# Exponentials over three PSUM banks, with two score buffers, in the attention stage that takes no maximum

## What is computed

```python
Q = (x @ W_k.T).reshape(B, S, H, dk).transpose(0, 2, 1, 3)
sq_norm = sum(Q * Q, axis=-1, keepdims=True)
scores = -(sq_norm - 2 * Q @ Q^T + sq_norm^T) / sqrt(dk)
attn = softmax(scores, axis=-1)
context_q = attn @ Q
```

## Time and profile before

| what | us |
|---|---|
| median of three runs | 1814.68 |
| lowest and highest run | 1811.52, 1815.87 |
| span of the profiled execution, first to last instruction | 1808.7 |
| TensorE busy in it | 1623.3 |
| ScalarE busy in it | 1295.9 |
| VectorE busy in it | 1230.8 |

### The profile page before, as it was taken

One profiled execution on the slowest core, in us unless ns is written; L12 is line 12 of the kernel. 1 busy time (PEld: TensorE's weight loads), 2 busy tenths in 40 slices (PEclk: granted clock), 3 DMA queues, 4 the chain that ended last, 5 costly groups with the idle time before them and its releaser, 6 DMA issues. The chain is left out here.

```text
span 1808.7 us, 39123 instructions
## 1 busy us (share of the span) xinstructions
PE 1623.3 (90%) x14558; PEld 775.2 (43%) x14558; DVE 1230.8 (68%) x2499; ACT 1295.9 (72%) x2201; POOL 362.4 (20%) x660
## 2 busy tenths in 40 slices
PE   7999896874899999989899999788866999999998
PEld 4676674751233333337533333255431333333356
DVE  4677777799899999947601111146767999999743
ACT  5555653794688888876689999667763888888863
POOL 4422423732000000014300000023420000000152
PEclk9889988885899999999989999899976999999999
DMA  4000000045222222200131111002242222222101
GB/s 125 1 1 1 1 1 1 1 142 183 68 77 79 72 73 78 79 6 19 48 95 57 56 56 56 1 22 69 74 122 81 57 58 61 63 59 57 30 7 42
DMA packets 115393, 98.52 MB, mean 54 GB/s; under 512 B 26763, under 2 KB 105413, under 8 KB 115205
## 3 DMA queue, kind: packets, MB, share of 16 engines
q1 hardware_dynamic: 114148, 95.68, 18.6%
q10 hardware_dynamic: 1056, 0.33, 0.1%
HBM read 63.82 MB, written 31.59 MB: 53 GB/s over the span
## 5 line engine op out<-in xcount | busy, mean ns | idle before, releaser
L1615 ACT ACTIVATE m_probs<-m_psum 128x512 f32<-128x512 f32 (+1 forms) x768 | 513.8, 758 | 97.7 <-PE m_psum L1532 92.7
L1615 ACT ACTIVATE e_probs<-e_psum 128x512 f32<-128x512 f32 x512 | 277.2, 597 | 85.6 <-PE e_psum L1532 80.6
L1659 DVE TENSOR_REDUCE a_minus_max<-e_psum 128x1 f32<-128x512 f32 x512 | 315.8, 684 | 19.6 <-PE e_psum L1541 18.3
L1659 DVE TENSOR_REDUCE a_minus_max<-m_psum 128x1 f32<-128x512 f32 x512 | 316.0, 684 | 18.0 <-PE m_psum L1541 16.4
L1532 PE MATMUL m_psum<-m_q_stack,m_k_stack 114*32 114x512 bf16 (+1 forms) x4096 | 295.7, 385 | 13.3 <-issue 6.9
L1552 PE MATMUL m_psum<-m_probs,m_v_ones 128*32 128x512 f32 x2048 | 271.0, 601 | 2.3 <-ACT m_probs L1615 1.6
L1532 PEld LDWEIGHTS m_psum<-m_q_stack,m_k_stack 114*32 114x32 bf16 (+1 forms) x4096 | 102.4, 96 | 218.2 <-issue 129.8
L1532 PE MATMUL e_psum<-e_q_stack,e_k_stack 126*32 126x512 bf16 x2048 | 159.0, 385 | 10.4 <-issue 8.3
L1504 POOL CAST a_max_parts<-a_minus_max 128x16 bf16<-128x16 f32 x64 | 12.6, 196 | 658.8 <-DVE a_minus_max L1659 658.8
L1552 PE MATMUL e_psum<-e_probs,e_v_ones 128*32 128x512 f32 x1024 | 133.7, 595 | 0.9 <-ACT e_probs L1615 0.8
L1541 PE MATMUL m_psum<-m_k_stack,m_q_stack 48*128 48x512 bf16 x512 | 113.4, 399 | 17.0 <-DVE a_minus_max L1659 16.9
(11 more groups left out here) (426 smaller groups left out, 2770.9 us busy)
## 6 DMA issues: line engine op xcount, KB each, us to landing
polar_q<-m_late SPq DMA_DIRECT2D x24, 256.0 KB, 3.0
polar_k<-m_late SPq DMA_DIRECT2D x24, 256.0 KB, 3.3
m_q_stack<-polar_q SPq DMA_DIRECT2D x64, 96.0 KB, 2.3
m_k_stack<-polar_k SPq DMA_DIRECT2D x64, 96.0 KB, 2.3
m_q_stack<-dist_parts SPq DMA_DIRECT2D x192, 32.0 KB
m_k_stack<-dist_parts SPq DMA_DIRECT2D x192, 32.0 KB
gate_parts<-e_late SPq DMA_DIRECT2D x24, 256.0 KB, 3.0
e_q_stack<-gate_parts SPq DMA_DIRECT2D x64, 72.0 KB
```

The costliest lines, as they stand in the source:

```text
L1615: act.activation(self.buf.probs[(NT * m + c) % self.buf.PROBS][:, self.WIDE * part:self.WIDE * (part + 1), :], self.ps_s[i % self.PAIRS], ...
L1659: dve.tensor_reduce(self.minus_max[n % 2][:, k:k + 1], ps[:, :], AX.X, ALU.max, negate=True).then_inc(self.bank_free, 1)
```

## The change

In `a5` alone, a unit becomes three tiles (1536 columns over three banks), counted on across chunks and groups: 170 units of three tiles and a last one of two, 171 in all. There are two score buffers of three banks (banks 4-6 and 0-2), the products go to bank 7, the turned context stays in bank 3. The scores of unit i wait for the exponential of unit i - 2. TensorE's order is now in `tensor_wide`: the scores of unit i, then the products of the chunk that ended in unit i - 2, if one did. The ring of exponentials keeps its twelve tiles, but as one tensor, so that a unit can lie across two chunks; ScalarE now waits for earlier products before each unit. `a3` and `a7` keep units of one tile and their order.

```diff
-        self.probs = [sb(f"probs{c}", [P, GH, T]) for c in range(self.PROBS)]
+        self.probs_row = sb("probs", [P, self.PROBS * GH, T])
+        self.probs = [self.probs_row[:, c * GH:(c + 1) * GH, :] for c in range(self.PROBS)]
...
-        self.WIDE = 1 if self.with_max else 2
-        self.PER = GH // self.WIDE
-        self.UNITS = self.PER * NT
+        self.WIDE = 1 if self.with_max else 3
+        self.PER = GH
...
+    def units_to(self, m):
+
+        return -(-self.TILES * m // self.WIDE)
...
-        wait_ge(sp, self.scores_done, self.UNITS * (n - self.buf.SLOTS + 1))
+        wait_ge(sp, self.scores_done, self.units_to(n - self.buf.SLOTS + 1))
...
+    def tiles_of_unit(self, i):
+        return range(self.WIDE * i, min(self.WIDE * (i + 1), self.TILES * self.N))
+
+    def unit(self, pe, i):
         wait_ge(pe, self.exp_done, i - self.PAIRS + 1)
...
+        for j, f in enumerate(self.tiles_of_unit(i)):
+            m, c, h = f // self.TILES, f // GH % NT, f % GH
+            g = m % self.buf.SLOTS
+            if not self.with_max and f % self.TILES == 0:
+                pe.wait_ge(self.loaded[g], 16 * self.LOADS * (m // self.buf.SLOTS + 1))
...
     def pv(self, pe, m, c):
-        pe.wait_ge(self.exp_done, self.UNITS * m + self.PER * (c + 1))
+        pe.wait_ge(self.exp_done, (self.TILES * m + GH * c + GH - 1) // self.WIDE + 1)
...
+    def products(self, pe, unit):
+
+        for chunk in range(NT * self.N):
+            if (GH * chunk + GH - 1) // self.WIDE == unit:
+                m, c = divmod(chunk, NT)
+                self.pv(pe, m, c)
+                if c == 1 and m >= 1 and m % 2 == 0:
+                    self.turn_ctx(pe, m - 1)
+
+    def tensor_wide(self, pe, m):
+        for i in range(self.units_to(m), self.units_to(m + 1)):
+            self.unit(pe, i)
+            self.products(pe, i - 2)
...
     def scalar(self, act, m):
-        for v in range(self.UNITS):
-            i = self.UNITS * m + v
-            c, part = divmod(v, self.PER)
+        RING = self.buf.PROBS * GH
+        for i in range(self.units_to(m), self.units_to(m + 1)):
+            tiles = self.tiles_of_unit(i)
             act.wait_ge(self.scores_done, i + 1)
-            if part == 0:
-                wait_ge(act, self.pv_done, NT * m + c - self.buf.PROBS + 1)
-            act.activation(self.buf.probs[(NT * m + c) % self.buf.PROBS][:, self.WIDE * part:self.WIDE * (part + 1), :],
-                           self.ps_s[i % self.PAIRS], ACT.Exp).then_inc(self.exp_done, 1)
+            if not self.with_max or i % GH == 0:
+                wait_ge(act, self.pv_done, (tiles[-1] - RING) // GH + 1)
+            at = tiles[0] % RING
+            act.activation(self.buf.probs_row[:, at:at + len(tiles), :], self.ps_s[i % self.PAIRS][:, 0:len(tiles), :], ACT.Exp).then_inc(self.exp_done, 1)
...
-        second = Attention(nc, sv, "a5", buf, psum, ((4, 6, 0), 2, (3,)), l1a_loads(sv), rows=6 * DH + 6, before=between)
+        second = Attention(nc, sv, "a5", buf, psum, ((4, 0), 7, (3,)), l1a_loads(sv), rows=6 * DH + 6, before=between)
...
-                    second.tensor(pe, s)
+                    second.tensor_wide(pe, s)
```

More of the change, by code:

```diff
@@ L1449, in bank_done @@
         else:
-            eng.wait_ge(self.exp_done, self.UNITS * self.N)
+            eng.wait_ge(self.exp_done, self.units_to(self.N))
+    def units_to(self, m):
+        return -(-self.TILES * m // self.WIDE)
     def context_done(self, eng, b):
@@ L1456, in stacks_done @@
     def stacks_done(self, eng):
-        eng.wait_ge(self.scores_done, self.UNITS * self.N)
+        eng.wait_ge(self.scores_done, self.units_to(self.N))
     def load(self, sp, n):
@@ L1519, in bank @@
         return self.ps_r[r % self.BANKS]
-    def unit(self, pe, m, v):
-        c, part = divmod(v, self.PER)
-        i = self.UNITS * m + v
+    def tiles_of_unit(self, i):
+        return range(self.WIDE * i, min(self.WIDE * (i + 1), self.TILES * self.N))
+    def unit(self, pe, i):
         wait_ge(pe, self.exp_done, i - self.PAIRS + 1)
@@ L1527, in unit @@
                 self.before.bank_done(pe, self.scores[i] + j)
-        g = m % self.buf.SLOTS
-        for j in range(self.WIDE):
-            h = self.WIDE * part + j
+        for j, f in enumerate(self.tiles_of_unit(i)):
[3 more added lines that the diff above has]
+                pe.wait_ge(self.loaded[g], 16 * self.LOADS * (m // self.buf.SLOTS + 1))
             for r in range(0, P, 32):
@@ L1568, in turn_max @@
         last.then_inc(self.bank_full, 1)
+    def products(self, pe, unit):
[9 more added lines that the diff above has]
+            self.products(pe, i - 2)
     def tensor(self, pe, s):
-        n, m, PER = s, s - self.LAG, self.PER
-        tiles = self.with_max and n < self.N
+        n, m = s, s - self.LAG
+        tiles = n < self.N
         if n < self.N:
             pe.wait_ge(self.loaded[n % self.buf.SLOTS], 16 * self.LOADS * (n // self.buf.SLOTS + 1))
-        if self.with_max and m >= 0:
+        if m >= 0:
             pe.wait_ge(self.rows_loaded, 32 * (m + 1))
         for c in range(NT):
-            for i in range(0, PER, 2):
+            for i in range(0, GH, 2):
                 if m >= 0:
-                    self.unit(pe, m, PER * c + i)
-                    self.unit(pe, m, PER * c + i + 1)
+                    self.unit(pe, self.TILES * m + GH * c + i)
+                    self.unit(pe, self.TILES * m + GH * c + i + 1)
                 if tiles and i == 0:
@@ L1584, in tensor @@
                         self.tile(pe, n, 4 * c + j)
-            if self.with_max and c == 1 and 1 <= s <= self.N:
+            if c == 1 and 1 <= s <= self.N:
                 self.turn_max(pe, s - 1)
@@ L1594, in tensor_end @@
     def tensor_end(self, pe):
-        self.pv(pe, self.N - 1, NT - 1)
+        if self.with_max:
+            self.pv(pe, self.N - 1, NT - 1)
+        else:
+            for unit in range(self.units_to(self.N) - 2, self.units_to(self.N)):
+                self.products(pe, unit)
         self.turn_ctx(pe, self.N - 1)
@@ L1608, in scalar @@
     def scalar(self, act, m):
-        for v in range(self.UNITS):
-            i = self.UNITS * m + v
-            c, part = divmod(v, self.PER)
+        RING = self.buf.PROBS * GH
+        for i in range(self.units_to(m), self.units_to(m + 1)):
+            tiles = self.tiles_of_unit(i)
             act.wait_ge(self.scores_done, i + 1)
-            if part == 0:
-                wait_ge(act, self.pv_done, NT * m + c - self.buf.PROBS + 1)
-            act.activation(self.buf.probs[(NT * m + c) % self.buf.PROBS][:, self.WIDE * part:self.WIDE * (part + 1), :],
-                           self.ps_s[i % self.PAIRS], ACT.Exp).then_inc(self.exp_done, 1)
-            if self.with_max and v == self.PER and m >= 1 and m % 2 == 0:
+            if not self.with_max or i % GH == 0:
+                wait_ge(act, self.pv_done, (tiles[-1] - RING) // GH + 1)
+            at = tiles[0] % RING
+            act.activation(self.buf.probs_row[:, at:at + len(tiles), :], self.ps_s[i % self.PAIRS][:, 0:len(tiles), :], ACT.Exp).then_inc(self.exp_done, 1)
+            if self.with_max and i - self.units_to(m) == GH and m >= 1 and m % 2 == 0:
                 self.evacuate(act, m - 1)
```

## The result

The changed kernel takes 1817.22 us (median of 20 runs, 1813.35 to 1821.19), the kernel before beside it 1814.49 (median of 20, 1804.11 to 1817.87). The ratio is 1.0018, with a 95% interval of 1.0009 to 1.0026: 3.3 us slower, 1.6 to 4.7. Fewer and longer exponentials made the kernel a little slower, as forecast, and by about the forecast amount; how much of that agreement is luck is said further down.

The account below looks back on a forecast made before the run. ACT was taken to bound most of a5, PE close behind. Terms -5.3 + 4.3 + 1.3 + 2.5 = +2.8 us on the 1808.7 us span, plus 6.0 us carried over to the median, gave 1817.5 us; range 1808 to 1824.

Parts of the forecast that it names:

- Fewer exponentials: ACT in a5: 171 exponentials in place of 256 save 0.062 us fixed part each, -5.3 us.
- Two buffers: Score buffers in a5: PE falls 0.53 us behind against 0.32 slack, four units take 5.41 or 5.55 us, +4.3 us.
- Transposes: PE in a5, 15 times: with smaller slack each delays the stage 0.67 us instead of 0.6, +1.3 us.
- copy: Pair boundaries in a5: products wait for VectorE's copy of the sums, ten of 15 stall PE 0.46 us, +2.5 us.
- added waits, ring and loads: a5: ACT's wait for products before every unit and later stack loads are already covered, 0 us.
- The start: Beginning of a5: bank waits move but are covered by the DMA that first scores await, 0 us.
- Six groups 46.5: Sign in a5: six groups should take 46.5 us.
- The 0.2 us of one exponential in four: Sign in a5's steady cycles: ACT should idle some 0.2 us before one exponential in four.
- scores would wait some 37 times: Sign in a5: PE's scores should wait for ACT some 37 times.
- A: Rival for a5: two buffers suffice and PE's own pace rules, -5.9 us, total 1808.8 us; chance 0.17.
- B: Rival for a5: each PE wait costs 0.1 us beyond its length, +7.6 us in all, total 1822.3 us; chance 0.14.
- C: Rival for ACT in a5: third bank costs like its own instruction, fixed part 0.124 us, +8.1, total 1822.8 us; chance 0.05.

Follow-up runs that it names:

- Two_tiles_two_buffers: Changed kernel with units of two tiles and only two score buffers of two banks; a5 267.7 us, total 1836.33 us in one run.
- bare kernels: a5's transposes, sum copies and divisions left out of the changed kernel (238.0 us) and of its version with two-tile units and three buffers (239.2 us).
- bare_wide: Changed kernel with a5's transposes, copies of the sums and divisions left out, three-tile units and two buffers kept; a5 238.0 us, total 1800.17 us.
- Two_tiles_two_behind: Changed kernel with two-tile units and three buffers again, sums in bank 2, new code kept; a5 248.4 us, ratio 1.0001 to the kernel before.
- sums_alternate: Changed kernel with each pair's sums in bank 7 or 3 by turns, so products skip the copy wait; a5 247.7 us, ratio 0.9979 to before.
- turn_in_gap: Changed kernel with the four transposes moved behind the scores of the next unit without products; a5 247.7 us, ratio 0.9976 to the kernel before.

## Why the prediction was right

Total: 1817.5 forecast, 1817.22 measured; a5 +2.8 forecast, +2.7 measured. The mechanism held: ACT saves its fixed parts, and two buffers, the transposes and the copy cost more than that. The closeness of the numbers is in part luck, as the parts show:

1. *Fewer exponentials, -5.3.* The fixed part stands: exponentials of 1536 columns add 1.344 and last 1.45 alone.
2. *Two buffers, +4.3.* Two_tiles_two_buffers shows that buffers bite. The two bare kernels give the sum of this term and the one above, -1.2 where -1.0 was forecast, and their rows of exponentials give this one alone, 4.2. The picture behind it was only half right: 5.41 us for four units was meant for undisturbed cycles and 5.55 for those after a disturbance. In bare_wide, where nothing disturbs, the two alternate to the end (steps of 1.34, 1.34, 1.34, 1.38 and 1.34, 1.34, 1.34, 1.51), so their mean held for another reason.
3. *Transposes +1.3 and copy +2.5.* Their sum is 13.3 - 9.3 = +4.0 by the bare kernels, +3.8 forecast. After the change each was priced well: transposes 9.7 measured and 15 x 0.67 = 10.05 forecast, copy 3.6 and 3.6. Two slips lie on the side of before. The 0.6 us of a pair (15.27 against 14.67) already holds whatever the copy cost, and 1.1 us for the copy was set beside it; the trace of before has 15 long steps of 1.52 us in place of 0.92, together 9.1 us, and behind the start no other loss. And 15 x (0.67 - 0.6) is 1.05, not 1.3. The first slip makes the sum too small by about 1 us, the second too large by about 0.3. How the 9.1 us of before divide between transposes and copy, no run shows.
4. *Cost 0 for added waits, ring and loads.* Two_tiles_two_behind, 248.4 against 248.5. The start was put at 0 too, and the changed kernel's was 0.5 us shorter. That shorter start, 11.40 us against 11.93, is what brings +3.3 down to the +2.7 that was measured. In the bare kernels, with the clock rising 8.1 to 8.2 us after the start in both, the wide one's start is only 0.2 us shorter (11.52 against 11.69), so most of the 0.5 probably goes with the earlier rise of the clock (7.75 us after the start against 8.42) and not with the change.
5. *What should be seen.* Six groups 46.5, measured 46.45; but 46.5 - 45.8 is +3.7 us over 32 groups and not +2.8, so the forecast held two numbers that do not agree, and behind the start the larger is nearer. Idle time of ACT of 0.46 behind transposes and 0.35 to 0.77 near pair boundaries: seen. The 0.2 us of one exponential in four are 0.04 and 0.17 by turns. a5 ended at 1154.35 and not near 1157, as it began 2.8 us earlier. One count was too low: scores would wait some 37 times. The profile counts 125 waits, on weight loads; counting units whose first matmul starts within 0.1 us of the exponential that frees their buffer gives 51 of 162.

The forecast total has its own share of luck: the totals of sums_alternate and turn_in_gap moved by 3 to 4 us more than their a5.

The rivals. A (TensorE's own pace, 1808.8) falls: it would make a5 5.9 us shorter, and a5 became longer; even the bare pipeline, with transposes and copies gone, takes 238.0 us where PE has 128 x 1.735 = 222 of own work. B (each wait costs 0.1 more) falls: a unit that waited starts its first matmul 0.053 us after the exponential's end and needs 0.45 us to its last matmul's start, one that did not wait 0.44. C (a fixed part per bank) falls by the 1.344.

The Trainium skill (page "ScalarE: Activation LUTs", section "What ACT_TABLE_LOAD costs") gives an activation 186 ns beside its columns and neighbours an overlap of about 93 ns. The 93 ns that this leaves for one in a row are not borne out by this case: steps of 0.490, 0.917 and 1.344 us for 512, 1024 and 1536 columns leave 0.062 to 0.064 us in all three.

## What to carry to other kernels

Before you make the bound engine's instructions longer, ask what they cost beyond their columns (here 0.062 us of 0.917) and what pays for it. If it is paid with a buffer, work out one turn of a buffer and the longest run of other work that comes between: the wave must fit into the slack, not only the mean. And where the bound engine's idle time hangs on an engine that has a little to spare per step, let that engine run further ahead, here by one unit, before touching the instructions; that one number was worth 8 us, and cost no memory. When a forecast agrees with the measurement, check its terms one by one all the same: here two slips and a shorter start brought the numbers closer together than the terms are.

## What was not expected

The length of a stage can be forecast much more sharply than the total can be measured: the ten lengths of a5 in the experiments came out within 1.2 us, eight of them within 0.5, and the two that missed by more did so in the start. The preparation of the last group, which no kernel here changes, takes 5 us more in some profiles than in others, at a granted clock of 0.90 instead of 0.98 between 1200 and 1300 us. The runs of sums_alternate suggest that the totals move with it, since the short ones had the higher mean clock. What sets it off is open.
